# One stream of attention scores across jobs, and an upper bound by ScalarE in place of mask matmuls for half of GpSimd's units

## The reference

```python
x = x + causal_attention(prior_attention(x))           # 16 heads of 16 each
x = x + moe_ffn(mixer(x))                              # gates, running means, layer norm; 8 experts, top 2, and a shared one
```

```python
bias = lam * where(prior_mask, 0, -1)
dense = softmax(scores + bias) @ V
sparse = softmax(where(index_mask, q . K[idx] * scale, -inf)) @ V[idx]
out = where(lam >= 1, sparse, dense) @ Wo.T + bo
```

## Time and profile before

| | |
|---|---|
| median of the runs | 1767.19 us |
| profiled execution | 1773.23 us, span of its trace 1771.4 us |
| busy share of the span | TensorE 91%, VectorE 52%, ScalarE 42%, GpSimd 36% |
| granted TensorE clock, mean | 0.949 of 2.4 GHz |
| prior attention, jobs 1 to 7 | 202 to 709 us |
| causal attention, jobs 8 to 15 | 709 to 1099 us |
| mixer of batch 1, experts, sum | 1099 to 1771 us |

### The profile page before, as it was taken

One profiled execution on the slowest core, in us unless ns is written; L12 is line 12 of the kernel. 1 busy time (PEld: TensorE's weight loads), 2 busy tenths in 40 slices (PEclk: granted clock), 3 DMA queues, 4 the chain that ended last, 5 costly groups with the idle time before them and its releaser, 6 DMA issues.

```text
span 1771.4 us, 20737 instructions
## 1 busy us (share of the span) xinstructions
PE 1615.1 (91%) x7584; PEld 771.1 (44%) x7632; DVE 916.6 (52%) x2045; ACT 741.7 (42%) x1028; POOL 642.8 (36%) x353
## 2 busy tenths in 40 slices
PE   5789899788989988979998898999998999999998
PEld 3423223223322322433443343555665566666655
DVE  6689688899658866546765732333312111111131
ACT  4744555455555555456645476133221111111111
POOL 5437889887888989021000000400002000000061
PEclk9569999999999999999999887999999999999999
DMA  3450213323131320344232112200040004243052
GB/s 104 143 142 19 67 33 76 84 59 92 44 77 31 68 49 7 76 134 114 62 85 61 32 60 90 87 2 1 1 142 8 17 4 169 86 150 109 15 106 37
DMA packets 75906, 121.45 MB, mean 69 GB/s; under 512 B 14920, under 2 KB 53265, under 8 KB 72731
## 3 DMA queue, kind: packets, MB, share of 16 engines
q1 hardware_dynamic: 72155, 113.62, 22.6%
q0 software_dynamic: 3072, 6.03, 2.0%
q10 hardware_dynamic: 576, 0.47, 0.1%
HBM read 85.08 MB, written 36.96 MB: 69 GB/s over the span
## 4 chain that ended last, share of the span: by engine, by line
PE 49%; DVE 5%; ACT 4%; issue 3%; DMA 3%; POOL 2%; SPq 2%; another core or an unknown queue 1%; ACTq 0%; DVEq 0%; POOLq 0%
PE wide L1967 19%; PE wide L1979 5%; PE wide L1985 5%; PE wide L1908 5%; PE wide L1885 3%; PE bank L1758 3%; POOL sb_prob L1090 2%; PE bank L1857 2%; DVE sb_rowmax L1563 2%; ACT sb_prob L1292 1%; DMA sb_den<-o_raw 1%; PE wide L1857 1%; PE bank L1750 1%; DMA parts<-sb_tables 1%; PE wide L1890 1%
## 5 line engine op out<-in xcount | busy, mean ns | idle before, releaser
L1090 POOL TENSOR_TENSOR sb_prob<-sb_prob,sb_weight 128x1024 f32<-128x1024 f32 x192 | 453.3, 2383 | 101.1 <-ACT sb_prob L1292 100.3
L1292 ACT ACTIVATE sb_prob<-wide 128x1024 f32<-128x1024 f32 (+3 forms) x384 | 347.7, 916 | 252.1 <-PE wide L1890 139.9
L1885 PE MATMUL wide<-sb_stack_q,sb_stack_k 99*128 99x512 bf16 (+3 forms) x896 | 295.8, 370 | 30.8 <-DVE sb_prob L1622 21.0
L1569 DVE CUSTOM_DVE_ANT_0 sb_junk<-bank,sb_bias 128x512 bf16<-128x512 f32 x339 | 225.6, 686 | 67.3 <-PE bank L1857 64.3
L1336 ACT ACTIVATE sb_sil<-wide 128x320 f32<-128x320 f32 (+1 forms) x128 | 66.2, 517 | 464.0 <-PE wide L1967 412.9
L1857 PE MATMUL bank<-sb_stack_k,sb_stack_q 96*128 96x512 bf16 (+3 forms) x596 | 217.8, 384 | 39.1 <-DVE sb_rowmax L1563 16.8
L1908 PE MATMUL wide<-sb_prob,sb_v_aug 128*17 128x512 f32 (+3 forms) x1792 | 229.7, 577 | 17.5 <-POOL sb_prob L1090 9.6
L1967 PE MATMUL wide<-sb_weight,sb_ffn 128*128 128x512 f32 x512 | 235.6, 604 | 0.0
L1714 DVE TENSOR_TENSOR sb_act_s<-sb_sil,wide 128x512 f32<-128x512 f32 x64 | 43.9, 686 | 273.2 <-ACT sb_sil L1336 242.4
L1563 DVE TENSOR_REDUCE sb_rowmax<-bank 128x1 f32<-128x512 f32 (+3 forms) x257 | 136.4, 554 | 76.5 <-PE bank L1860 45.8
L1967 PE MATMUL wide<-sb_xgT,sb_big 128*128 128x320 f32 x512 | 152.8, 444 | 1.1 <-ACT sb_xgT L1351 1.1
(11 more groups left out here) (258 smaller groups left out, 1940.8 us busy)
## 6 DMA issues: line engine op xcount, KB each, us to landing
sb_stack_k<-parts SPq DMA_DIRECT2D x32, 256.0 KB, 7.0
o_raw<-sb_o_raw SPq DMA_DIRECT2D x32, 256.0 KB, 2.1
sb_big<-rg SPq DMA_DIRECT2D x8, 1024.0 KB, 5.1
sb_big<-ru SPq DMA_DIRECT2D x8, 1024.0 KB, 7.2
sb_big<-rd SPq DMA_DIRECT2D x8, 1024.0 KB, 9.7
sb_stack_q<-parts SPq DMA_DIRECT2D x16, 384.0 KB, 5.1
parts<-sb_o_norm SPq DMA_DIRECT2D x48, 128.0 KB
sb_stack_q<-parts SPq DMA_DIRECT2D x16, 256.0 KB, 5.5
```

Source lines behind the costliest of these rows:

```text
L1090: e.tensor_tensor(p, p, weight_of(*u[1:]), ALU.mult).then_inc(weigh_p.handle, 1)
L1292: e.activation(p[:, :, first:HALF], sc[:, :, first:HALF], ACT.Exp).then_inc(SC.empty_sem(u), 1)
L1569: e.tensor_tensor_reduce(out=junk[:, i % 2], in0=BK.tile(u)[:], in1=bias[:, qt, lo:hi], scale=1.0, scalar=-3e38, op0=ALU.add, op1=ALU.max, ...
L1885: i = e.matmul(sc[:, j * HALF + first:(j + 1) * HALF], stack_k[0:ROWS_M, n % 3, g, kt * P:(kt + 1) * P], stack_q[0:ROWS_M, n % 3, g, half ...
```

## The change

Three things change.

1. *One stream.* `attention_plan` no longer closes a job before the next begins. It walks one queue of all jobs' units; the products stay four units behind, so a job's last products and its last "o" stand among the next job's first five units. Loads and extras of the job before begin behind them (`opened`), and a new batch's values at the fifth unit. The FFN loads move from job 15's fifth unit to behind its last score.
2. *Bound by ScalarE.* In units 1, 4 and 7 of eight (`BOUND_UNITS`, half of GpSimd's) the mask matmuls fall away. ScalarE computes `r = relu(1 - s)` and then `exp(1 - r)`, which is `exp(min(s, 1))`, and the weight 0 does the masking.
3. *Tables later.* A bias table of batch 1 now stands before the eight maxima of job 4 that use it, and these are ordered by it; "kw" and "kw_sum" come one unit later.

```diff
+BOUND_UNITS = (1, 4, 7)
+def bounded(n, u):
+    return to_pool(n, u) and u % 8 in BOUND_UNITS
...
 def with_tables(steps):
...
         out.append(("kb", 1, t))
         if t + 2 < NT:
             out.append(("kb_load", 1, t + 2))
-        out += steps[NH * t:NH * (t + 1)]
-    return out + steps[NH * NT:]
+        out += [u for u in steps if u[3] == t]
+    return out
...
+def behind_job(n):
+    att, b, q = JOBS[n]
+    loads, units = [], []
...
+    stage = STAGES[q]() if att and b and q in STAGES else []
+    if q % 2 and n + 1 < len(JOBS):
+        gap, later = (stage[:len(stage) // 2], stage[len(stage) // 2:]) if stage else (GAP, GAP)
+        units += [("num", att, b, q // 2)] + gap + [("inv", att, b, q // 2)] + later + [("times", att, b, q // 2)]
+    else:
+        units += stage
+    if q == NQ - 1 and n + 1 < len(JOBS):
+        units += GAP + outputs(att, b)
+    return loads, units
...
 def attention_plan():
-    for n, (att, b, q) in enumerate(JOBS):
...
+    queue = [(n, u) for n in range(len(JOBS)) for u in range(units_of(n))]
+    for i in range(len(queue) + PV_LAG):
+        n, u = queue[i] if i < len(queue) else (len(JOBS) - 1, units_of(len(JOBS) - 1) + i - len(queue))
...
+            opened = ends[PV_LAG] if n else 0
...
-        steps = [(0.9 * k / len(extras), 0, k, f) for k, f in enumerate(extras)]
+            steps = [(opened + (0.9 - opened) * k / len(extras), 0, k, f) for k, f in enumerate(extras)]
...
-            if n + 1 == len(JOBS) and u == PV_LAG:
-                plan += [("ffnload", k) for k in range(EARLY)]
+        if i == len(queue):
+            plan += [("ffnload", k) for k in range(EARLY)]
+        if u == (PV_LAG + 1 if n else 0):
+            plan += loads
+        if u >= PV_LAG or not n:
             plan += values[:2 if causal else 1]
...
-            while steps and (u >= last or steps[0][0] < ends[u]):
+        while steps and (u >= last - 1 or steps[0][0] < ends[u]):
...
+        if i >= PV_LAG:
+            m, v = queue[i - PV_LAG]
+            half, kt, pair = place(m, v)
+            if pair == PAIRS_OF - 1:
+                plan.append(("pv", m, half, kt))
+                if JOBS[m] == (0, 0, NQ - 1):
+                    late += [(i, ("kw_load", 1, kt, half)), (i + 3, ("kw", 1, kt, half)), (i + 4, ("kw_sum", 1, kt, half))]
...
+            elif kt == 0 and (m or half):
+                plan.append(("o", m, 0) if half else ("o", m - 1, 1))
...
@@ GpSimd
                 elif u[0] == "score" and to_pool(*u[1:]):
                     p = prob_tile(u[1:])
-                    w.wait_ge(SC.emptied(u))
+                    w.wait_ge(exp_b.after(u[1:]) if bounded(*u[1:]) else SC.emptied(u))
...
@@ ScalarE
+                    if bounded(n, v):
+                        one = v_aug[:, 0, 0, DH:DH + 1]
+                        w.wait_ge(const_done.end)
+                        e.activation(p, sc, ACT.Relu, bias=one, scale=-1.0).then_inc(SC.empty_sem(u), 1)
+                        w.wait_ge(SC.emptied(u))
+                        e.activation(p, p, ACT.Exp, bias=one, scale=-1.0).then_inc(exp_b.handle, 1)
+                        continue
...
@@ TensorE
-                    if to_pool(n, v):
+                    masked = to_pool(n, v) and not bounded(n, v)
+                    if masked:
                         w.wait_ge(cut_d.end)
                         w.wait_ge(unlisted_a.after((0, kt, half)))
...
-                                     start=True, stop=not diag and not to_pool(n, v))
-                        if to_pool(n, v):
+                                     start=True, stop=not diag and not masked)
+                        if masked:
                             i = e.matmul(sc[:, j * HALF:(j + 1) * HALF], cut[:, JOBS[n][1]],
```

98 lines of the change are left out of this document (44 added, 54 removed).

## The result

| | before | after |
|---|---|---|
| median of the runs | 1768.43 us | 1781.24 us (1778.16 to 1786.99) |
| ratio, 95% interval | | 1.0067 (1.0043 to 1.0091) |
| profiled execution | 1773.23 us | 1786.99 us, span 1785.2 us |
| granted clock of TensorE, mean | 0.949 | 0.936 |

The forecast was 1742 us with a range of 1712 to 1767; the change costs some 12 us instead of giving 25.

The account below looks back on a forecast made before the run. The prediction took no engine as full and sought the gain in GpSimd's idle 76.9 us of jobs 1 to 7. Terms 24 + 13 - 2 - 7 - 5 = 23, plus 2 for job 0, gave 25 us: 1742 us, range 1712 to 1767.

Parts of the forecast that it names:

- One stream: At the seven borders of jobs 0 to 7, GpSimd's 29.7 us of gaps go: 24 us gain.
- the stream gives little: Rival: border gaps return as waits inside jobs and causal waits come in full; some 8 us gain, 1759 us; chance 0.17.
- 192 mask matmuls gone: TensorE loses 42 us of work in units 1, 4 and 7, recovering about half of GpSimd's eligible inner gaps: 13 us gain.
- the clock: Slower rival: fewer masks thin out TensorE in jobs 0 to 7 and its clock falls, costing 25 us; chance 0.02.
- ScalarE's bound: Two activations in 96 units, 119 us more on ScalarE, covered nearly everywhere: loss 2 us, bounds 0 and 15.
- VectorE held: Two more of VectorE's 16 maxima-finishing instructions in jobs 0 to 7 held by GpSimd, 3.5 us each: loss 7 us.
- held at every finish: Slower rival: VectorE's finishing step of the maxima held in all 16 places, 45 us more, near 1782 us; chance 0.08.
- all of GpSimd's idle goes: Rival: GpSimd alone in front, jobs 1 to 7 take 444 instead of 507 us, near 1705 us; chance 0.18.
- The causal jobs: Jobs 8 to 15: a 1.6 us wait for the row of maxima at up to seven borders; loss 5 us.
- extras squeezed: Divisions, outputs, products and mixer steps squeezed by 17% in jobs 0 to 7, 24% in causal jobs; 0 to 8 us.
- Tables later: Some four bias tables move from job 2 into job 3 and six maxima back: about even, 1 us at most.
- FFN loads: The six loads issue some 20 us later, landing near 1090 us before first use at 1099.14: no cost.

Follow-up runs that it names:

- e1: The changed kernel without ScalarE's bound, all mask matmuls kept; ratio 1.0021 to the kernel before.
- e9: The kernel before with stream and later tables in jobs 0 to 7 only, causal jobs in old order, no bound; 11.7 us under the kernel before.
- e6: The kernel before without the mask matmuls of units 1, 4 and 7, one exponential each, output not the reference's; 0.3 us gain.
- e5: The kernel before, all masks kept, with two ScalarE activations in units 1, 4 and 7; ratio 1.0090, 15.8 us lost.
- e12: The kernel before, masks kept, with three small ScalarE activations behind the exponential of units 1, 4 and 7; ratio 1.0020, 3.5 us lost.
- e2: The kernel before with only the bound on units 1, 4 and 7 and their masks gone, old plan and tables; ratio 1.0108.
- e8: The changed kernel itself, measured again on the chip of later runs; ratio 1.0064 to the kernel before.
- e4: The changed kernel with GpSimd waiting, before its second-last multiplication ahead of a finishing step, until VectorE has done that step; 0.7% under the changed kernel.
- e10: e9 with e4's GpSimd wait added; ratio 0.9912, 15.6 us under the kernel before.
- e7: The kernel before with e4's GpSimd wait added in jobs 0 to 7; ratio 1.0045, 8 us slower.
- e11: The changed kernel with the division's reciprocal four pauses later in causal jobs without mixer steps; ratio 1.0027 to the kernel before.
- e3: The changed kernel with the second batch's tables in their old places; 12 to 13 us under the changed kernel by the ratios.

## Why the prediction was wrong

*"One stream: 24 us gain."* The seven gaps went as forecast: in e1 GpSimd's idle time ahead of the multiplications fell by 24.1 us. The step that failed is what stands next in line: 17 us came back ahead of the splits. I had listed it, as the rival "the stream gives little", and given it 0.17. Measured, stream and tables in jobs 0 to 7 are worth 11.7 us by the ratio (e9), half the forecast.

*"192 mask matmuls gone: 13 us gain."* Failed. e6 gives 0.3 us, with an interval of about 3.5 either way. The row said that TensorE isn't the floor; I then let half of GpSimd's inner gaps depend on it all the same, without a row that showed TensorE's work as what they waited for. The idle times of the earlier trace rows end with an exponential, and e6 shows that fewer matmuls ahead of it don't bring it earlier, with the clock at 0.94 instead of 0.97. The rival "the clock" named this fall, but not its price: e6 is level, where it had 25 us of loss.

*"ScalarE's bound: loss 2 us, bounds 0 and 15."* The durations held (1.109 and 1.149 us for 1.11 and 1.15); ScalarE's busy time grew by 106 us, for 119 forecast. The step that failed is the cover: the delay of a unit was not under a queue on GpSimd. e5 measures 15.8 us, just outside the bounds, of which e12 leaves some 4 to ScalarE's time. Masks and bound together cost 19 us on the order before (e2), 8 on the stream (e8 against e1, 1.0064 and 1.0021, intervals overlapping), where I had a gain of 11.

*"VectorE held: two more, loss 7 us."* Four of jobs 0 to 7 are now held 5.5 to 6.5 us, instead of three of 6.5 to 7.3. Their length is about even in sum (the eight from 150 to 700 us average 3.9 us, 3.7 before). What changed is less the number than the cost of each, since a product and its split now stand behind some: freeing VectorE gains in a streamed order (e4, and e10 by its trace) and loses in the old one (e7). The slower rival, "held at every finish", had the right engine and the wrong count. It was also mis-added: 45 and 5 us against 37, with 2 and 8 on top, give a time near 1790, not 1782. And what the rival "all of GpSimd's idle goes" had against it, four engines over 70% busy, holds for three: ScalarE was busy 308.05 of 559 us, 55%.

*"The causal jobs: loss 5 us."* The sign was right and the mechanism nearly absent: a wait for the row of maxima shows ahead of one causal job only, 1.28 us before job 15's first score (1.26 in the other full streams). The step that failed is *"extras squeezed"*, which I had left out of the sum as 0 to 8 us in the range: the reciprocal comes too early, 6.5 us by e11, and batch 0's transposes in job 15, 4.4 us by the traces, of 15 in all (e1 against e9).

*"Tables later: 1 us at most."* I hadn't seen one wait: in job 2 VectorE waits for a table's load that SyncE issues behind the division's transfers, and TensorE waits behind it, with the clock at 0.50 for the next 10.2 us.

```profile
309.70 2.73 DVE L1638 TENSOR_SCALAR sb_bias<-sb_tables,sb_flags 128x1024 bf16<-128x1024 bf16 x1 [3.93 <-DMA sb_tables<-count_qk]
...
313.36 0.61 PE L1891 MATMUL bank<-sb_stack_k,sb_stack_q 96*128 96x512 bf16 x1 [6.49 <-DVE sb_rowmax L1603]
```

That wait stands in e3 as well (3.9 us) and in every other streamed kernel (2.8 to 4.5 us), and in none with the old order, so it is the stream's order, not the tables' place. All ten streamed kernels lose 3.6 to 8.1 us between the copies of jobs 2 and 3; that this wait is the reason isn't shown. What the tables' place itself costs stays open: by e3's ratio it is far more than 1 us, by its trace 3.5 in jobs 0 to 7. *FFN loads: 0* holds: nothing waits for them.

One way to split the loss, by the ratios: stream in jobs 0 to 7 -11.7, stream in the causal jobs +15.4, masks and bound on top +7.6, together +11.3. These are differences along the chain before, e9, e1, e8, so that their sum is e8's own 1.0064 by construction and checks nothing; by way of e3 the same loss would be put down to the tables.
